# Casting batch 3's x later: behind the casts of the transposed attention rows

## What is computed

```
Q = relu(x Wq' + bq) * decay;  K = relu(x Wk' + bk) * decay;  V = x Wv' + bv      (16 heads of 16)
KV = K' V;  Ksum = sum_n K;  Z = 1 / (Q Ksum + 1e-6);  out = (Q KV) * Z           (linear attention)
x1 = layernorm(x + out Wo' + bo)
probs = softmax(x1 w_gate); top 2 of 8 experts, weights normalised to sum 1
routed = sum over the 2 of w * (silu(g) * u) w_down[e],  [g u] = x1 w_gate_up[e]  (inner width 128)
shared = (silu(g) * u) w_sh_down,                        [g u] = x1 w_sh_gate_up  (inner width 512)
result = layernorm(x1 + routed + shared)
```

## Time and profile before

| quantity | value |
|---|---|
| median of 3 runs | 237.13 us |
| the three runs | 237.13, 240.16, 234.39 us |
| time of the profiled execution | 235.75 us |
| its span, first to last instruction | 233.9 us |
| busy: PE, DVE, ACT, POOL | 219.4, 151.7, 117.6, 133.9 us |
| mean granted TensorE clock | 0.99 of full speed |
| the chain that ended last, by engine | PE 58%, DVE 17%, DMA 9%, ACT 5% |

### The profile page before, as it was taken

The page is one execution under the profiler, slowest core; times in us unless marked ns, Lnnn a source line. Parts: engine busy times, 40 slices in busy tenths (PEclk is TensorE's granted clock), DMA queues, the critical chain, the costliest instruction groups (busy, mean ns, idle before and its releaser), DMA issues.

```text
span 233.9 us, 5040 instructions
## 1 busy us (share of the span) xinstructions
PE 219.4 (94%) x1440; PEld 192.5 (82%) x1440; DVE 151.7 (65%) x534; ACT 117.6 (50%) x304; POOL 133.9 (57%) x153
## 2 busy tenths in 40 slices
PE   7999999989989989999999899999999999999980
PEld 2478888879878978978899688999999998889780
DVE  2862463445866584865989866666666652399984
ACT  2282522680375173257315266777777764412563
POOL 0057687799878978577677006666677774003020
PEclk9999999999999999999999999999999999999996
DMA  5964573333131122023164336556666620396046
GB/s 159 367 234 104 151 262 92 92 91 90 48 90 55 40 90 92 0 93 113 68 219 146 80 86 177 161 167 176 182 181 175 179 78 3 124 390 205 0 151 212
DMA packets 21580, 31.72 MB, mean 136 GB/s; under 512 B 3248, under 2 KB 14257, under 8 KB 21556
## 3 DMA queue, kind: packets, MB, share of 16 engines
q1 hardware_dynamic: 17552, 22.46, 32.3%
q0 software_dynamic: 3456, 8.43, 10.3%
q10 hardware_dynamic: 548, 0.53, 0.7%
HBM read 19.70 MB, written 12.76 MB: 139 GB/s over the span
## 4 chain that ended last, share of the span: by engine, by line
PE 58%; DVE 17%; DMA 9%; ACT 5%; SPq 4%; issue 4%; POOL 1%; POOLq 0%; DVEq 0%
PE bank L336 11%; PE bank L338 11%; PE bank L337 10%; DVE x L1276 4%; PE bank L636 3%; PE bank L378 3%; PE bank L537 3%; DMA o_sb<-x_slots 3%; DMA xt_raw<-in_xT 2%; PE bank L456 2%; SPq L291 2%; PE bank L663 2%; DVE xt_raw L1085 2%; PE bank L666 2%; PE bank L664 2%
## 5 line engine op out<-in xcount | busy, mean ns | idle before, releaser
L1439 POOL DMA_INDIRECT y_pairs<-x_t,dst x40 | 38.9, 973 | 30.8 <-DVE dst L1170 25.1
L1402 POOL DMA_INDIRECT x_slots<-x,slot x32 | 32.3, 1011 | 10.1 <-issue 9.0
L336 PE MATMUL bank<-x1t_hi,wf_hi 128*128 128x512 f32 x64 | 26.3, 411 | 0.7 <-DVE xt_raw L1085 0.5
L336 PE MATMUL bank<-wf_hi,ot_hi 128*128 x80 | 25.8, 322 | 0.0
L338 PE MATMUL bank<-x1t_hi,wf_lo 128*128 128x512 f32 x64 | 25.3, 395 | 0.0
L337 PE MATMUL bank<-x1t_lo,wf_hi 128*128 128x512 f32 x64 | 25.2, 394 | 0.0
L1383 POOL TENSOR_TENSOR wf_lo<-stage,wf_hi 128x512 fp32r<-128x512 f32 x18 | 23.2, 1289 | 1.4
L338 PE MATMUL bank<-wf_hi,ot_lo 128*128 x80 | 22.6, 282 | 0.0
L337 PE MATMUL bank<-wf_lo,ot_hi 128*128 x80 | 22.4, 280 | 0.0
L752 ACT ACTIVATE k_sb<-bank,cst 128x256 f32<-128x256 f32 x16 | 7.7, 480 | 29.2 <-PE bank L353 27.2
L1170 DVE SCALAR_TENSOR_TENSOR dst<-o_sb,te_f 128x1 f32 (+1 forms) x40 | 8.8, 219 | 17.0 <-ACT ot_hi L866 17.0
(11 more groups left out here) (185 smaller groups left out, 689.3 us busy)
## 6 DMA issues: line engine op xcount, KB each, us to landing
o_sb<-x_slots SPq DMA_DIRECT2D x40, 129.0 KB
stage<-in_wffn SPq DMA_DIRECT2D x18, 256.0 KB, 2.9
x<-in_x SPq DMA_DIRECT2D x4, 512.0 KB, 7.2
out<-x SPq DMA_DIRECT2D x8, 256.0 KB, 2.4
xt_raw<-in_xT SPq DMA_DIRECT2D x3, 512.0 KB, 6.3
x_slots<-fill SPq DMA_DIRECT2D x9, 129.0 KB, 2.9
x<-in_watt SPq DMA_DIRECT2D x4, 256.0 KB, 5.9
k_sb<-y_pairs SPq DMA_DIRECT2D x2, 512.0 KB, 4.5
```

The costliest lines, as they stand in the source:

```text
L336: mm(o, w_hi, m_hi, start=start, stop=False, **more)
L1402: pool.indirect_dma_start(out=x_scat, out_offset=bass.IndirectOffsetOnAxis(ap=slot[:, j, t:t + 1], axis=0), in_=x1[:, t, :], in_offset=Non ...
L1439: pool.indirect_dma_start(out=y_scat, out_offset=bass.IndirectOffsetOnAxis(ap=dst[:, j:j + 1], axis=0), in_=ey[:, u, :], in_offset=None, b ...
```

## The change

In the loop of ScalarE's program the cast of batch 2's x, in the iteration of batch 0, stays where it was. The cast of batch 3's x, in the iteration of batch 1, moves from ahead of the query evictions to behind the casts of the transposed attention rows, ahead of `x1f_out(0)`. No instruction is added or removed, and no other engine's list changes.

```diff
                 if b >= 1:
                     x1_apply(b - 1)
-                if b + 2 < NB:
+                if b == 0:
                     split_x_hi(b + 2)
-                if b == 0:
                     q_out(b + 1, [0])
                     ot_hi_out(b)
                     q_out(b + 1, [1])
                 else:
                     q_out(b + 1)
                     ot_hi_out(b)
-                if b >= 1:
+                    if b == 1:
+                        split_x_hi(b + 2)
                     x1f_out(b - 1)
```

## The result

| kernel | runs | median us | lowest, highest us |
|---|---|---|---|
| before | 4 | 235.99 | 234.39, 240.16 |
| changed | 4 | 239.20 | 237.38, 240.21 |

The changed kernel is 1.4% slower: ratio 1.0137 with the interval 1.0073 to 1.0201, 3.2 us. The interval lies above 1 and reaches just past the 2% bound. The forecast was 238.0 us in a range of 235.3 to 240.8, so the time lies inside; the size of the step, 0.5%, was too small.

A forecast was written before the change was run, and what follows sets the result against it. The prediction took GpSimd's list, through batch 2's norm step, to bound the kernel late in the run. TensorE's gain counted 0 and GpSimd's lag +1.15, so 236.86 + 1.15 = 238.0 us, range 235.3 to 240.8.

The forecast's parts named there:

- the gate: Last iteration: TensorE's line 445 waits 0.59 us for ScalarE's normalisation of batch 2, which waits for GpSimd's norm step.
- What GpSimd loses: GpSimd's subtraction of batch 3's x waits for the moved casts, starting at 50.08 instead of 48.93: 1.15 us late.
- TensorE's gain at the first line 445: Iteration of batch 1: earlier query evictions let line 445 start at 48.14 instead of 48.67, about 0.52 us gained.
- The gain is worth nothing at the end: TensorE reaches the gate 0.52 us earlier but stands there, already 0.59 us early: term 0.
- When the casts end: ScalarE, iteration of batch 1: the moved casts end at 50.00 instead of 47.38, 2.62 us later.
- The lag goes whole to the gate: GpSimd's list from batch 3's subtraction to line 232 takes nothing back; the whole 1.15 us arrives.
- covers named in the prediction: Slack ahead of later uses: 0.13 us covered by 3 us, batch 3's x and batch 1's norm by 4 us each.
- TensorE's idle time at the gate: Wait before line 445 in the last iteration: 0.59 + 0.52 + 1.15 = 2.26 us.
- No slack behind the gate: Everything after these transposes moves with them, so the lag reaches the end whole: +1.15 us.
- GpSimd is late anyway: Rival: chunk loads usually bring GpSimd to batch 3's subtraction after 50.08, so no lag; 236.9 us, chance 0.15.
- The gate was never GpSimd's: Rival: another owner, or the lag is made up, leaving only TensorE's gain: -0.52, 236.3 us, chance 0.05.
- The clock falls in the new gap: Rival: TensorE's clock halves after the 2.26 us wait, costing 2 us beyond the 1.15; 240.0 us, chance 0.08.

The follow-up runs named there:

- f3_before: The kernel before, unchanged, profiled again on chip C: 261.70 us in that execution, median of the kernel before there 258.99 us.
- h1_before: The kernel before, unchanged, a single profiled run on chip D: 261.78 us.
- g3_norm_first: Changed kernel, GpSimd's batch 3 subtraction behind the next two chunks and batch 2's norm ahead of batch 1's x1 subtraction, chip A: 234.60 us, 1.0015 to before.
- g1_after: The changed kernel run again, nothing else altered, on chip A: 237.48 us, ratio 1.0144 to the kernel before.
- e5_heat: Changed kernel plus ten matmuls with unused product in TensorE's gap ahead of the x1 transposes, chip B: 262.99 us, ratio 1.0014 to the kernel before.
- f1_after: The changed kernel run again, nothing else altered, on chip C: 259.31 us, ratio 1.0015 to the kernel before.
- e1_after: The changed kernel run again, nothing else altered, on chip B: 262.87 us, ratio 1.0005 to the kernel before.
- h2: Kernel before, batch 3's casts put ahead of batch 2's K and V evictions, batch 2's norm ahead of batch 1's x1 subtraction, chip D: 258.61 us, ratio 0.9974.
- g2: Changed kernel with GpSimd's batch 3 subtraction moved behind the next two chunks, chip A: 236.25 us, ratio 1.0077 to the kernel before.
- f2: Kernel before plus one small unused GpSimd power operation ahead of batch 3's subtraction, chip C: 260.02 us, ratio 1.0031 to the kernel before.
- e2: Changed kernel with GpSimd's batch 3 subtraction moved behind the next two chunks, chip B: 260.72 us, ratio 0.9947 to the kernel before.
- f4: Changed kernel, batch 3's subtraction behind the next two chunks, batch 2's norm ahead of batch 1's x1 subtraction, chip C: 258.65 us, ratio 0.9921 to before.

## Why the prediction came out as it did

The way was right: the moved casts delay GpSimd, its list carries the delay to the gate, and the kernel is slower. The term that was mis-sized is the 1.15 us under "What GpSimd loses".

- **TensorE's gain at the first line 445: right.** Forecast 48.14 without a wait, measured 48.30 without a wait. Against the earlier trace rows it is 0.37 and not 0.52, because ScalarE's normalisation and the Q product ended 0.1 later in this execution.
- **The gain is worth nothing at the end: right in result, half right in its reason.** The text said that the gate was already late for TensorE. In f3_before and h1_before it is not: TensorE arrives at 82.31 and 82.59 and does not wait. It is the changed kernel's own lag that swallows the gain. And g3_norm_first, where the lag is gone, shows no gain at the end either (ratio 1.0015).
- **When the casts end: right.** 50.00 forecast, 50.15 measured; the subtraction at 50.23 (forecast 50.08), 50.12 in g1_after, 50.31 in e5_heat, 50.36 in f1_after, 50.58 in e1_after.
- **GpSimd's lag: the term that was mis-sized.** "I take 1.15, since the rows show its arrival" rests on 48.93 of the earlier trace rows. Up to that instruction GpSimd's list is the same in every kernel here, so all fourteen traces show when it was free: 47.90 (h2), 47.97 (g2), 48.05 (f1), 48.07 (f3), 48.15 (the first profile of the change), 48.15 (h1), 48.25 (f2), 48.46 (e2), 48.50 (f4), 48.51 (g3), 48.92 (g1), 48.98 (before), 48.99 (e1) and 49.21 (e5). The trace that the forecast was read from is the third latest. GpSimd's wait for the casts in the five traces in which it has to wait for them was 2.08, 1.58, 1.09, 2.30 and 1.20 us (after, e1, e5, f1, g1): the 1.15 is among them, at the low end. From the middle arrival, 48.4, to the mean start of the five, 50.3, it is 2.0 us.
- **The lag goes whole to the gate: right.** 1.30 more at line 1373 than in the earlier trace rows (50.23 against 48.93) is 1.32 at line 232 (82.30 against 80.98) and 1.31 at line 445 (84.67 against 83.36). None of the covers named in the prediction broke, and none took anything back.
- **TensorE's idle time at the gate: 2.26 forecast, 2.56 measured** (2.55 to 2.59 in g1, f1 and e1). Where GpSimd is early, the kernel before starts line 445 when TensorE arrives: 82.31 and 82.59 on chips C and D, and 82.77 would be the arrival in the earlier trace rows. The changed kernel's 84.51 to 84.86 is 1.7 to 2.6 us later, against 1.15 forecast. No trace of the kernel before with an early GpSimd was taken on chip A.
- **No slack behind the gate: right on the fast chip,** 32.2 us in both kernels, for a line 445 at 83.2 or later; ahead of that 0.4 us are lost again, as g3_norm_first shows. At the experts' first tile the load of the scattered rows makes 0.2 more of it.
- **The sum.** The price of 1.7 to 2.6 is below the medians, 3.1 to 3.2 apart, and near the lowest runs on chip A, 236.30 against 233.61, 2.7 apart. What remains, 0.5 to 1.5 us, is not settled. One candidate is the granted clock, as worked out above. Another is the expert tiles' waits for x rows: in g1_after TensorE waited 3.1 us in all for them, in the first profile of the change 1.3, in before 1.4, in g3_norm_first 0.9. That is one execution each, and no experiment varied it.
- **The rivals.** *GpSimd is late anyway* is refuted: in none of the fourteen traces was it free after 49.21, where 50.08 was needed. *The gate was never GpSimd's* is refuted by g2 and g3 on chip A, where only its list changes and the time follows; for the kernel before it would have been true in two of its three traces, and the change made the gate GpSimd's. *The clock falls in the new gap*: it fell in e1_after, e2_lo_later and f2_lag. On chip A it is open. Its step of 3.15 us (1.15 of lag and 2 of clock) has the size of the measured 3.2, with a lag term that was too small; that agreement doesn't show the clock.

That 238.0 lies only 1.2 us below the measured time is in part luck. The step was too small by 2 us, and the base, the average of four shown times, 236.86, was 0.9 above the 235.99 that the kernel before measured; with that base the same working gives 237.1. The range held because it was made wide enough for the spread of the runs and for the clock; its lower end, 235.3, is higher than its own working reaches (236.3 less 2 us).

## What to carry to other kernels

When a cast or an eviction is moved to a later place, ask first which in-order engine has its partner near the front of its list: here a move that gained 0.4 us on ScalarE and TensorE made GpSimd wait 1.1 to 2.3 us, which showed only 34 us later. Read the arrival of that partner from more than one execution where transfers lie ahead of it: a margin taken from one profile (1.55 us here, where the other traces put it between 0.5 and 1.8) can be far from the usual one. And where the mover wants only to get an instruction out of the way, look for idle time ahead of it before placing it behind.

## What the runs showed of the hardware that was not expected

- **The granted clock did not do the same after the same gap.** In e1_after TensorE stood 2.59 us, ran the eight matmuls of line 445 in 1.53 us and then eight of line 392 in 2.02 (1.09 each at full speed), and was back at 1.00 at 89 us. In f1_after and g1_after it stood 2.55 and 2.57 us and read 1.00 throughout; in e2_lo_later it fell after 2.02. In both the fall came only when TensorE had resumed: the reading is 1.00 from 84 to 85 us in e1_after, whose line 445 starts at 84.86. So the 2.1 us read from the program's end is no fixed limit. The Trainium skill (TensorE: Matmul & The Clock Gate, section "What's actually happening") says that activity releases the throttled state; e1_after agrees with that, as the half-speed stretch ended during dense matmuls. What decides whether it is entered stays open here.
- **Chips differ by 10%.** Chips B, C and D take 259 to 263 us for a program that takes 234 to 236 on A. Their traces run alike to the gate (line 777 at 82.48 in f1_after, 82.54 in the profile of the change); f1_after is then 5.7 us later at line 1128, 7.8 at the first expert tile and 20.9 at the last. ScalarE and VectorE wait longer for TensorE's results, beyond the end of the recorded matmuls, as in the row with 4.97 us for "remote" above (a release for which the profile names no instruction), and TensorE then waits for VectorE in turn. TensorE's waits in f3_before (what it waited for, us in total, times, longest us), then in g1_after:

```profile
PE bank L654 <- DVE b_row L1182: 9.3, 9, 1.5
PE bank L470 <- DVE hot_m L1074: 5.4, 1, 5.4
```

```profile
PE bank L636 <- DMA o_sb<-x_slots: 3.1, 4, 1.2
PE bank L445 <- ACT x L777: 2.6, 1, 2.6
```

  In most of these traces the granted clock read 1.00 from the gate to 110 us, so it doesn't explain the first of these stalls. Later, TensorE waits 5.3 to 5.6 us at line 470 for VectorE's line 1074 (at most 0.2 us in the traces at chip A's speed), and the clock fell to 0.50 in that wait in all nine traces of chips B, C and D, to be back at 1.00 by 128 us, which adds to the difference. The cause of the stalls is open. The verdict on a change of this size depends on the chip: 1.4% on A, nothing measurable on B and C.
